# Reordering the experts' choice, the prefix sums, the gate's power and the slab fills in a macaron block with a token-mixing layer

## What is computed

```python
x = x + 0.5 * ffn(layernorm(x))       # stage route a, experts a
x = x + attn(layernorm(x))            # stage mix_and_route
x = x + 0.5 * ffn(layernorm(x))       # routing in mix_and_route, experts b

# ffn: 16 experts, each token goes to its two best, at most 1280 tokens per expert
logits = x2d @ router_w.T + router_b
vals, idx = top_k(logits, 2); gates = softmax(vals)
pos = cumsum(one_hot(idx)) - 1        # a token's place within its expert
kept = pos < capacity                 # then scatter, two products with gelu, weighted gather

# attn: RWKV-6, 4 heads of 64
xx = shifted(x) - x
lora = tanh((x + xx * maa_x) @ maa_w1)            # five mixes of x and xx from it
r, k, v = xr @ Wr, xk @ Wk, xv @ Wv
g = tanh(xg @ gate_w1) @ gate_w2
w = exp(-exp(time_decay + tanh(xw @ decay_w1) @ decay_w2))
S = w * S + k v^T;  y = r (S + u k v^T)           # along the tokens, per head
out = (groupnorm(y) * ln_g + ln_b) * g @ Wo
```

## Time and profile before

| what | value |
|---|---|
| median of 3 runs | 3041.12 us (3040.53 to 3043.16) |
| profiled execution, its own time | 3043.45 us |
| its span | 3041.6 us |
| TensorE matmul busy | 2764.8 us (91%) |
| VectorE busy | 1997.8 us (66%) |
| ScalarE busy | 1575.5 us (52%) |
| GpSimd busy | 1265.8 us (42%) |
| stretch 0 to 236 us (constants, route) | TensorE 117.94, VectorE 122.95, GpSimd 128.02 us busy |
| stretch 236 to 1190 us (experts a, the first mixing work behind it) | TensorE 906.97 us busy |
| stretch 1302 to 2090 us (mixing steps) | TensorE 731.40, VectorE 656.88, GpSimd 557.43 us busy |

### The profile page before, as it was taken

One profiled execution on the slowest core, in us unless ns is written; L12 is line 12 of the kernel. 1 busy time (PEld: TensorE's weight loads), 2 busy tenths in 40 slices (PEclk: granted clock), 3 DMA queues, 4 the chain that ended last, 5 costly groups with the idle time before them and its releaser, 6 DMA issues. The chain is left out here.

```text
span 3041.6 us, 63629 instructions
## 1 busy us (share of the span) xinstructions
PE 2764.8 (91%) x21994; PEld 2212.3 (73%) x21994; DVE 1997.8 (66%) x4620; ACT 1575.5 (52%) x2733; POOL 1265.8 (42%) x1072
## 2 busy tenths in 40 slices
PE   6536999999999995899999999984999999999997
PEld 6535888888888883466666666663888888888886
DVE  5545666666666652688989898864666666566664
ACT  5424666666665652344444444432666656656663
POOL 2671322322222223457777777753222222232233
PEclk9999999999999997999999999997999999999998
DMA  9925545545544526201111111014455445445444
GB/s 343 334 94 116 91 81 89 94 77 88 95 78 86 96 33 222 98 16 44 35 53 33 54 33 55 26 38 116 82 89 95 77 86 95 79 86 94 80 70 149
DMA packets 540965, 281.28 MB, mean 92 GB/s; under 512 B 397591, under 2 KB 503131, under 8 KB 540480
## 3 DMA queue, kind: packets, MB, share of 16 engines
q1 hardware_dynamic: 478624, 202.67, 26.8%
q0 software_dynamic: 57888, 75.16, 14.6%
q10 hardware_dynamic: 4224, 0.52, 0.1%
HBM read 150.83 MB, written 146.41 MB: 98 GB/s over the span
## 5 line engine op out<-in xcount | busy, mean ns | idle before, releaser
L763 POOL DMA_INDIRECT acc_a<-ae_ob,ae_to x160 | 260.8, 1630 | 675.0 <-ACT ae_ob L712 623.0
L763 POOL DMA_INDIRECT acc_b<-be_ob,be_to x150 | 242.7, 1618 | 637.3 <-ACT be_ob L712 578.7
L730 ACT ACTIVATE be_h<-be_pH,b 128x512 f32<-128x512 f32 (+1 forms) x384 | 236.8, 617 | 359.2 <-PE be_pH L657 337.5
L730 ACT ACTIVATE ae_h<-ae_pH,b 128x512 f32<-128x512 f32 (+1 forms) x384 | 236.7, 616 | 342.1 <-PE ae_pH L657 324.1
L1478 POOL TENSOR_TENSOR m_xf<-m_tmp,m_xT 128x512 f32<-128x512 f32 x160 | 174.9, 1119 | 151.6 <-DVE m_tmp L1185 85.1
L1529 POOL DMA_INDIRECT slots_b<-m_row,m_sidx x128 | 143.1, 1118 | 109.3 <-issue 106.2
L1788 PEld LDWEIGHTS m_PP<-m_RP,m_KS 64*64 64x64 f32 x6656 | 115.6, 134 | 87.5 <-issue 86.4
L464 POOL DMA_INDIRECT slots_a<-ar_row,ar_sidx x128 | 126.0, 984 | 99.7 <-issue 73.8
L1788 PE MATMUL m_PP<-m_RP,m_KS 64*64 64x64 f32 x6656 | 130.0, 221 | 26.5 <-DVE m_A L1215 26.3
L657 PE MATMUL ae_pH<-ae_xT0h,ae_w_0h 128*128 128x512 f32 (+1 forms) x256 | 87.8, 343 | 69.3 <-DVE ae_xT0l L839 65.5
L1185 DVE SCALAR_TENSOR_TENSOR m_tmp<-m_B,m_ch,m_xx 128x512 f32<-128x512 f32 x160 | 114.0, 741 | 48.8 <-PE m_B L1895 38.5
(11 more groups left out here) (347 smaller groups left out, 9007.8 us busy)
## 6 DMA issues: line engine op xcount, KB each, us to landing
ae_stage<-in_w SPq DMA_DIRECT2D x64, 512.0 KB, 3.6
be_stage<-in_w SPq DMA_DIRECT2D x64, 512.0 KB, 3.5
slots_a<-empty SPq DMA_DIRECT2D x5, 4160.0 KB, 25.0
slots_b<-empty SPq DMA_DIRECT2D x5, 4160.0 KB, 31.6
ae_xq<-slots_a SPq DMA_DIRECT2D x252, 64.0 KB, 2.7
be_xq<-slots_b SPq DMA_DIRECT2D x252, 64.0 KB, 2.7
ar_xin<-in_x SPq DMA_DIRECT2D x16, 512.0 KB, 10.0
m_xin<-acc_a SPq DMA_DIRECT2D x16, 512.0 KB, 4.6
```

What stands on the lines that cost most here:

```text
L730: t = act.activation(dst[:, 0:SIZES[b]], pH[c % 2][:, 0:SIZES[b]], ACT.Gelu, bias=S.b1[:, bass.ds(i * (2 * FC) + (u * FC + f), 1)])
L763: pool.indirect_dma_start(S.acc[tag][:, :], bass.IndirectOffsetOnAxis(ap=to[m][:, q:q + 1], axis=0), ob[m][:, q, :], None, bounds_check=T ...
```

## The change

Routing stage: SyncE's queue has four loads, three fills, two loads, two fills, then the other loads, where loads and fills alternated from the fourth load on. `logits` and `copy_turned` handle the group that was turned one step earlier.

Mixing stage: VectorE's `choose` goes from ahead of the level-5 decays to behind `gated`, and `places` from ahead of the first two mixes to behind them. GpSimd's `root_spread` goes ahead of `gate`. ScalarE's tanh of the rest goes ahead of `assemble_left`, and `shares` behind the copy of the turned outputs. TensorE's `low_rest` goes ahead of level 7 and `prefix` behind the first output product.

```diff
--- before.py
+++ after.py
@@ -205,11 +205,15 @@
                         sp.wait_ge(xn_ready, g - XRING + 1)
                     sp.dma_start(xin[g % XRING][:, :, :], x_grp[g]).then_inc(x_loaded[g % XRING], 16)
 
-                for g in range(XRING):
+                for g in range(4):
                     load(g)
-                    if XRING - PAIRS <= g:
-                        S.empty_rows(sp, tag, g - (XRING - PAIRS))
-                for g in range(XRING, NG):
+                for j in range(3):
+                    S.empty_rows(sp, tag, j)
+                for g in range(4, 6):
+                    load(g)
+                for j in range(3, PAIRS):
+                    S.empty_rows(sp, tag, j)
+                for g in range(6, NG):
                     load(g)
                 for dst, src in S.mix.loads:
                     sp.dma_start(dst, src).then_inc(weights_loaded, 16)
@@ -415,8 +419,8 @@
                         turn(s + 3)
                     if 0 <= s + 1 < NG:
                         prefix(s + 1)
-                    if 0 <= s + 3 < NG:
-                        logits(s + 3)
+                    if 0 <= s + 2 < NG:
+                        logits(s + 2)
 
             @block.scalar
             def _(act):
@@ -441,7 +445,8 @@
                 for s in STEPS:
                     if 0 <= s + 3 < NG:
                         normalise(s + 3)
-                        copy_turned(s + 3)
+                    if 0 <= s + 2 < NG:
+                        copy_turned(s + 2)
                     if 0 <= s + 1 < NG:
                         g = s + 1
                         act.wait_ge(dif_ready, g + 1)
@@ -1433,18 +1438,20 @@
                     keep(L, 5)
                     if live(K) and not live(L):
                         gated(K)
-                    if live(R):
+                    if live(R) and not live(L):
                         choose(R)
                     factors(L, 5)
                     keep(L, 6)
                     if live(K) and live(L):
                         gated(K)
+                    if live(R) and live(L):
+                        choose(R)
                     factors(L, 6)
-                    if live(R) and live(L):
-                        places(R)
                     if live(X):
                         for m in range(2):
                             mix_in(X, m)
+                    if live(R) and live(L):
+                        places(R)
                     if live(K):
                         add_out(K, 0)
                     if live(X):
@@ -1565,8 +1572,8 @@
                         for m in range(8, 10):
                             mix_add(F, m)
                     if live(K) and live(L):
+                        root_spread(K)
                         gate(K)
-                        root_spread(K)
                     if live(Z):
                         scatter(Z, (1,))
                     if live(L):
@@ -1740,18 +1747,19 @@
                     if live(F):
                         values(F)
                         queries(F)
-                    if live(R):
+                    if live(R) and not live(L):
                         shares(R)
                     if live(X):
                         low(X, "LA", lora[:, :])
+                        low(X, "LG", lorag[:, :])
                     if live(L):
                         assemble_left(L)
-                    if live(X):
-                        low(X, "LG", lorag[:, :])
                     if live(K):
                         filled(act, "O1", K - 1)
                         filled(act, "L", R)
                         untie(YG, K, ygT[:, :, :])
+                    if live(R) and live(L):
+                        shares(R)
                     if live(L):
                         assemble(L)
 
@@ -2059,13 +2067,11 @@
                         level(L, 6)
                     if live(X):
                         low(X)
-                    if live(R) and live(L):
-                        prefix(R)
+                    if live(X):
+                        low_rest(X)
                     idle_last(L, 2)
                     if live(L):
                         level(L, 7)
-                    if live(X):
-                        low_rest(X)
                     if live(K) and not live(L):
                         idle_behind(4)
                     if live(K):
@@ -2079,6 +2085,8 @@
                         level(F, 0)
                     if live(K):
                         output(K, 0)
+                    if live(R) and live(L):
+                        prefix(R)
                     if live(X):
                         mixes_of(X, range(2, 4))
                     if live(K):
```

## The result

The changed kernel takes 3056.84 us, median of 5 runs (3053.07 to 3061.32), beside 3041.12 for the kernel before (5 runs, 3038.15 to 3043.16): ratio 1.0051, 95% interval 1.0037 to 1.0066. The forecast was 3046.4 us, range 3035 to 3054. The sign was right and the size wrong: +15.7 us in place of +5.3. The profiled execution took 3055.47 us.

What follows compares the result with a forecast made beforehand. The prediction took the mixing step to be bound by a ring through four engines and routing by GpSimd's scatters; routing -2.9 and mixing +8.2 us made +5.3 on 3041.12, so 3046.4 us, range 3035 to 3054.

Steps and rivals of the forecast that it cites:

- Routing, -2.9 us: Routing stage: two loads fewer ahead of the fifth fill, so the 112 scatters end 2.9 us earlier.
- Power does not block: Mixing stage: GpSimd's power doesn't hold up VectorE's decay; if it did, +13.0 us in all, chance 0.05.
- The gate's cost of 0.33 us: Mixing stage: the gate, now behind the power, meets the first level-5 decay and costs 0.33 us, 3.6 us in all.
- Rest takes the place of the 1.61 us wait: TensorE ahead of level 7: the rest product (1.05 us) fills the wait for VectorE's `m_A`; priced at nothing on the ring.
- any rival: Alternatives: GpSimd slack, 3033.4 us, chance 0.18; small effects, 3042.5, 0.17; routing gains nothing or power blocks, 3049.3 or 3054.1, 0.17.
- the new wait ahead of turning: TensorE ahead of turning the gated rows: a wait of about 1 us expected in the changed kernel's profile.
- Choice and gate, 0.64 us per step: VectorE's choice behind the gated outputs, with the gate's delay, makes each of eleven steps 0.64 us longer, 7.0 us in all.
- `m`: VectorE's first mix of the coming group: forecast at 1629.20 against 1628.56 before; a later one means a longer step.
- ring: Mixing step closes through four engines, with GpSimd packed for 12.86 us up to its four mix additions; eleven steps close it.
- The second output product, forecast 0.4 us earlier: TensorE in the mixing step: this product starts at 1631.2 against 1631.63, which isn't on the ring.
- Ends, +1.4 and -0.2: Mixing stage outside the eleven steps: steps 14 and 15 cost +0.9 and +0.5 us, steps 0 to 2 about -0.2.

Runs made afterwards that it cites:

- filled: Changed kernel with one more 128x256 product, its result unused, behind the prefix on TensorE: 3054.61 us, ratio 1.0032; ten steps 520.0 us.
- two kernels not edited there: Kernel before with only the choice, places, prefix and shares moved, 3050.52 us; routing part alone plus dummy products in the second to last step, 3048.04 us.
- the routing part with the last step filled: Routing part alone plus dummy products (3, 2 and 2 of 128x512) in three TensorE waits of the second to last step: 3048.04 us, ratio 1.0011.

## Why the prediction was wrong

**Routing, -2.9 us: right.** The scatters began 3.56 us earlier, the routing part alone gave 2.0 us in the median. Nothing became late; the interval, -0.2 to 0.0%, holds both 2.0 and 2.9.

**Power does not block: right** on the rows (0.70 us beside a power of 3.31). The gate's cost of 0.33 us for the first level-5 decay is there (1.00 us in place of 0.69). Power alone was worth +3.6 by my sum and +3.3 measured, but my place for it was wrong: before the choice moves, the gate hits the choice itself, that is absorbed, and the ten steps don't grow. Of the loss the one profile shows 1.9 us, in the last steps. By the Trainium skill, "SBUF — State Buffer", section "Who interferes with whom", the power should have held the decay up; the changed kernel and the one with the power alone show 0.70 us (0.71 in the last two) beside it in all 15 steps, and the measurement decides.

**"Rest takes the place of the 1.61 us wait": the step that failed most.** I priced it at nothing. Alone it costs 0.29% (0.17 to 0.41), 9.2 us in the median. With the rest alone the wait ahead of level 7 doesn't vanish, it splits: 0.44 us ahead of level 7, and 1.12 to 1.23 ahead of turning the gated rows, where it was at most 0.23. In the changed kernel it is gone, and 0.76 us ahead of turning and 0.65 ahead of the third mix, in the mean of the ten steps, stand in its place. The forecast had named the new wait ahead of turning, of about 1 us, and gave it no price. TensorE has the same work and about the same idle time (1.6 to 1.7 us a step in the mean of the ten, 1.7 before), but falls to half clock behind the new waits in some executions and steps, and in the first step in every one profiled: +3.1 us in the first two steps of the rest alone, +3.0 for each of the ten steps that has it. That TensorE's clock could change had no term in my sum at all, in any rival.

How much of a median is clock can be estimated from the mean clocks. In the kernel before 0.001 of it goes with 1.5 to 2.0 us (last section). The rest alone has 0.976 in the median beside 0.980, so 6 to 8 of its 9.2 us; the mixing part alone has 0.976 beside 0.979, so 4.5 to 6 of its 15.1 us. These are estimates and no experiment.

**Choice and gate, 0.64 us per step: mis-sized a little.** Counted from the start of level 6 (1620.70), `m` is 10.22 us later; before it was 1628.56 - 1618.93 = 9.63, and the forecast was 10.27. So `m` was right in this step. The ten steps still grew by 10.2 us and not 6.4: 3.0 of it is the half clock (filled: 520.0), and 7.2 is ring. The ring's 0.64 a step came to 0.72, which accounts for 0.8 us of what the forecast missed, and the ring theory stands as far as lengthening goes. As a picture of what sets the pace before it was incomplete, since a shorter ring gives nothing. The second output product, forecast 0.4 us earlier, is where it was: 12.73 us behind the start of level 6, beside 12.70 before. By the ring it doesn't count.

**Ends, +1.4 and -0.2: too small.** From step 14 to 15 alone +4.6 us. The waits for choice, prefix and `places` are as named (0.47 us), but output products priced at the duration of the earlier trace rows took 7.5 us in place of 5.3, at half clock. The early steps, where I expected -0.2, gave +1.5 and +1.8, at half clock behind the wait of 1.09 us: this too goes with the rest, in 12 profiles of 12, and 2 of the other 6 have it as well, behind a wait of 0.93.

The Trainium skill, page "TensorE: Matmul & The Clock Gate", section "A second HAM failure mode: psum-queue depth-cycling", tells of a kernel in which short idle times between groups of matmuls make the clock swing between its two levels. The trace agrees: no wait of the ten steps is over 1.0 us in the changed kernel, nor over 1.25 with the rest alone, and the clock falls in one step and not in the next. What it doesn't tell is why waits of 1.61 us in before, at another place, brought no fall. I had read the clock of the earlier trace rows, 1.00, as given; it belonged to that order of work with its waits.

**What stays open.** What the second limit at 51.05 and 51.5 us is made of. Why the same wait brings the half clock in one execution and not in another, and why it came in the first step in two kernels not edited there. Why the routing part with the last step filled is slower than without, at the same mean clock. How many steps at half clock a typical execution of the rest alone has: the three profiled had one, none and one, and the difference to the median is argued from the mean clocks. The ring's share and the clock's of the 15.7 us are known for one execution, not for the median.

## What to carry to other kernels

In a stretch with TensorE busy 96%, idle time was not only a number to bring down: moved to another place at about the same length, it went with falls of the clock. Before moving work to fill one wait, list every wait that is left behind it with its new length, and price each at half clock for the products that follow. A ring with no slack can cost what is added to it (here 0.7 us a step for 0.6), even where taking time out of it gives nothing, because something else of the same length lies beside it. And where a kernel's executions spread, set each beside its mean clock before reading one profile as typical.

## What the runs showed of the hardware

- Over 35 executions of the kernel before, the span goes with the mean granted clock: 3034.3 us at 0.982, 3047.5 at 0.977, about 2 us for each 0.001 (correlation -0.91). One program, 13 us of spread. The three other sets of executions of this kernel (25, 28 and 15) give 1.5 to 1.7 us for each 0.001, with correlations of -0.80 to -0.86.
- A fall to half clock in one of the ten mixing steps makes that step 1.6 to 3.2 us longer than the same step without it (in the changed kernel the step behind it was 0.6 to 0.7 shorter): an output product of 8 matmuls takes 3.1 to 3.8 us in place of 1.99.
- A GpSimd power of 128x16 (3.31 us) doesn't hold up VectorE's 128x512 decay beside it (0.70 us), a gate of 128x1024 (2.34 us) holds up even a cast of 128x8, 2.39 us in place of 0.17. The Trainium skill, "SBUF — State Buffer", section "Who interferes with whom", names casts among the VectorE operations that can contend with GpSimd when their operands meet certain conditions; the trace agrees for this one.
- A dummy product of 128x512 with the identity took 1.0 us on TensorE, in two records of 0.5 each; I had taken 0.45 for a product, which in the projections' rows is the time of one record.
